# Local attention in blocks of 64 queries by 96 keys, with a step of 32 slots

## The reference

```python
qkv = x @ Wqkv                                   # 128 -> 3 * 1024, 16 heads of 64; x is token-shifted
q = l2norm(q) * qs;  k = l2norm(k) * ksc         # then rotary tables with a scale per token
# local attention, window 32: query i sees keys i-32 .. i
mask = (it < jb) | (it > jb + w) | (jb == -1)
sim = einsum('bhwie,bhwje->bhwij', bq, bk2) * QK_SCALE
attn = softmax(where(mask, -big, sim), -1)
out = einsum('bhwij,bhwje->bhwie', attn, bv2)
x = x + out @ Wo
# feed-forward: layernorm, W1 (128 -> 2 * 341), a * gelu(gate), W2, residual
```

## Time and profile before

| | |
|---|---|
| median of three runs | 5323.7 us |
| profiled execution, span | 5323.2 us |
| PE, DVE busy | 4734.5 us (89%), 4646.5 us (87%) |
| ACT, POOL busy | 3909.8 us (73%), 3520.9 us (66%) |
| phase A, B, C (about) | 0 to 508, 508 to 4600, 4600 to 5323 us |

### The profile page before, as it was taken

The page is one execution under the profiler, slowest core; times in us unless marked ns, Lnnn a source line. Parts: engine busy times, 40 slices in busy tenths (PEclk is TensorE's granted clock), DMA queues, the critical chain, the costliest instruction groups (busy, mean ns, idle before and its releaser), DMA issues. The chain is left out here.

```text
span 5323.2 us, 107258 instructions
## 1 busy us (share of the span) xinstructions
PE 4734.5 (89%) x32878; PEld 3336.2 (63%) x32878; DVE 4646.5 (87%) x8811; ACT 3909.8 (73%) x11543; POOL 3520.9 (66%) x2504
## 2 busy tenths in 40 slices
PE   6996899989999899999999999999989999688887
PEld 4554666666666666666666666666667666445553
DVE  4776999989999999999999999999989999388887
ACT  2554787878778787787778877787878878577774
POOL 0111777778778777777777777787878788145454
PEclk9998999999999999999999999999999999888888
DMA  1000000000000000000000000000000000000000
GB/s 23 6 5 27 1 1 1 0 7 8 9 1 0 6 8 9 1 0 6 8 9 0 1 4 10 9 0 1 0 14 3 0 0 0 5 3 3 3 3 5
DMA packets 35433, 26.55 MB, mean 5 GB/s; under 512 B 11203, under 2 KB 29190, under 8 KB 35078
## 3 DMA queue, kind: packets, MB, share of 16 engines
q1 hardware_dynamic: 26302, 22.22, 1.4%
q10 hardware_dynamic: 8776, 0.45, 0.1%
HBM read 20.56 MB, written 2.10 MB: 4 GB/s over the span
## 5 line engine op out<-in xcount | busy, mean ns | idle before, releaser
L1286 POOL TENSOR_TENSOR b_w<-b_w,b_vt 128x512 f32<-128x512 f32 x768 | 1176.2, 1536 | 850.8 <-DVE b_ss L1196 542.7
L1290 POOL TENSOR_TENSOR b_rn<-b_ssm,all_neg_half 128x16 f32<-128x16 f32 x384 | 1128.1, 2938 | 32.0
L1085 ACT ACTIVATE b_Pr<-ps,b_nm 128x128 f32<-128x128 f32 x1536 | 570.3, 371 | 523.9 <-DVE b_nm L1250 522.9
L1244 DVE TENSOR_TENSOR b_Pr<-b_Pr,b_rinv 128x640 f32<-128x640 f32 x768 | 738.0, 961 | 26.4
L965 PE MATMUL ps<-b_Whi,b_xlo 128*128 128x512 f32 x1152 | 578.3, 502 | 202.3 <-DVE b_vt L1194 166.1
L1250 DVE TENSOR_REDUCE b_nm<-ps 128x4 f32<-128x640 f32 x768 | 628.9, 819 | 58.4 <-PE ps L946 50.8
L1106 ACT ACTIVATE b_sq<-ps 128x512 f32<-128x512 f32 x768 | 471.4, 614 | 259.6 <-PE ps L967 210.4
L1087 ACT ACTIVATE b_Pr<-ps,b_nm 128x160 f32<-128x160 f32 x1536 | 610.3, 397 | 0.0
L1192 DVE TENSOR_TENSOR b_w<-ps,until_b_rotab 128x512 f32<-128x512 f32 x768 | 523.9, 682 | 20.4 <-ACT b_sq L1106 17.5
L1194 DVE TENSOR_TENSOR b_vt<-ps,until_b_rotab 128x512 f32<-128x512 f32 x768 | 522.5, 680 | 0.0
L1196 DVE TENSOR_REDUCE b_ss<-b_sq 128x8 f32<-128x512 f32 x768 | 519.2, 676 | 0.0
(11 more groups left out here) (269 smaller groups left out, 11969.3 us busy)
## 6 DMA issues: line engine op xcount, KB each, us to landing
b_Wraw<-in_L_ffn_Wqkv SPq DMA_DIRECT2D x36, 256.0 KB, 2.8
b_Wo<-in_L_ffn_Wo SPq DMA_DIRECT2D x6, 512.0 KB, 4.2
a_xtok<-in_L_attn_hidden_states SPq DMA_DIRECT2D x16, 128.0 KB, 2.1
out<-c_xout SPq DMA_DIRECT2D x16, 128.0 KB, 1.8
b_W<-in_L_ffn_W SPq DMA_DIRECT2D x6, 341.0 KB, 2.9
setup_wmod<-in_L_wmod SPq DMA_DIRECT2D x2, 384.0 KB
b_W<-in_L_ffn_W SPq DMA_DIRECT2D x6, 128.0 KB
setup_rot<-in_rot SPq DMA_DIRECT2D x1, 256.0 KB
```

What stands on the lines that cost most here:

```text
L1085: nc.scalar.activation(s.Pr[:, p % 4, j, 0, WIN:], ps[:, S_BANK[j], WIN:KEYS], ACT.Exp, bias=s.nm[:, h, 0:1], accum_out=s.ssum[:, h, 0:1])
L1244: nc.vector.tensor_tensor(rows, rows, inverse, ALU.mult).then_inc(s.scaled, 1)
L1286: nc.gpsimd.tensor_tensor(rows, rows, s.vt[:, i % 4], ALU.add).then_inc(s.pool_add, 1)
L1290: nc.gpsimd.tensor_tensor(s.rn[:, j], s.ssm[:, j], g.neg_half[:, 0:HB], ALU.pow).then_inc(s.pool_r, 1)
```

## The change

The attention is tiled as four blocks of 64 queries by 96 keys (BLK = 64, KEYS = 96) instead of two of 128 by 160. Two pairs of heads make a round; an item has 4 rounds. Masks and scores go to 64x64 corners of the PE array: head j picks the row half and the S bank, block b the column half and the partitions of PSUM. Maximum, reciprocal and multiplication are one instruction a round, over 768 columns. The DVE transpose is gone; each block's 96 keys are transposed whole by PE. As a block's keys now need their values on partitions 0 to 95, V is held by block: ACT copies a piece into Vraw and SP spreads it by transfers, 10 an item. V has one buffer instead of two. SP's program becomes part of the stepped loop, with its weight loads in it. A step has SLOTS = 32 slots, and all slot tables of phase B are new. Phase C's source is the same.

```diff
+BLK = 64
+KEYS = BLK + WIN
+NBLK = NT // BLK
+MASK_COLS = 2 * TT * KEYS
...
+ROUNDS = HPAIRS // 2
+HALF = INNER // 2
+SLOTS = 32
+ROUND = SLOTS // ROUNDS
+QK_SLOT = {0: (0, 0), 3: (0, 2), 6: (1, 0), 8: (1, 2), 15: (0, 1), 17: (0, 3), 22: (1, 1), 24: (1, 3)}
+V_SLOT = {14: (0, 4), 20: (1, 4), 29: (0, 5), 31: (1, 5)}
...
+SCORE_LAG, EXP_LAG, SCALE_LAG, TURN_LAG, VALUE_LAG, COPY_LAG = 0, (2, 5), 8, (9, 11), 15, 14
...
+            def spread_values(item, half, tt):
+                cols = slice(half * HALF, (half + 1) * HALF)
+                sp.wait_ge(s.act_front, N_PIECES * item + PIECE.index(VALUE[2 * half + tt]) + 1)
+                if tt == 0 and not (isinstance(item, int) and item == 0):
+                    sp.sem_inc(s.spent, 1)
+                    sp.wait_ge(s.pv_done, ROUNDS * (item - 1) + 2 * (half + 1))
+                if tt == 0:
+                    sp.dma_start(s.V[WIN:KEYS, 0, cols], s.Vraw[0:BLK, tt]).then_inc(s.v_in[tt], 16)
+                    sp.dma_start(s.V[0:KEYS, 1, cols], s.Vraw[BLK - WIN:P, tt]).then_inc(s.v_in[tt], 16)
+                    sp.dma_start(s.V[0:WIN, 2, cols], s.Vraw[P - WIN:P, tt]).then_inc(s.v_in[tt], 16)
+                else:
+                    sp.dma_start(s.V[WIN:KEYS, 2, cols], s.Vraw[0:BLK, tt]).then_inc(s.v_in[tt], 16)
+                    sp.dma_start(s.V[0:KEYS, 3, cols], s.Vraw[BLK - WIN:P, tt]).then_inc(s.v_in[tt], 16)
...
+                def scores(r):
...
+                    for b in range(2):
+                        for j in range(2):
+                            side, block = slice(j * DB, (j + 1) * DB), slice(b * BLK, (b + 1) * BLK)
+                            nc.tensor.matmul(ps[block, S_BANK[j], 0:MASK_COLS], g.ident_bf[side, side], g.mask_bf[side, b], start=True, stop=False,
+                                             skip_group_check=True)
+                    for a in range(2):
+                        q, k = s.qkT[:, pa, 2 * r + a], s.qkT[:, pa, INNER // P + 2 * r + a]
+                        for tt in range(TT):
+                            for b in range(2):
+                                start = tt * P + b * BLK
+                                hidden = WIN if start == 0 else 0
+                                at = (a * TT + tt) * KEYS + hidden
+                                for j in range(2):
+                                    side = slice(j * DB, (j + 1) * DB)
+                                    last = nc.tensor.matmul(ps[b * BLK:(b + 1) * BLK, S_BANK[j], at:at + KEYS - hidden], q[side, start:start + BLK],
+                                                            k[side, start - WIN + hidden:start + BLK], start=False, stop=True, skip_group_check=True)
...
+                def values(item, r):
...
+                    for a in range(2):
+                        for blk in range(NBLK):
+                            for j in range(2):
+                                head = slice((4 * r + 2 * a + j) * DB, (4 * r + 2 * a + j + 1) * DB)
+                                at = j * TT * P + blk * BLK
+                                last = nc.tensor.matmul(ps[j * DB:(j + 1) * DB, O_BANK, a * NT + blk * BLK:a * NT + (blk + 1) * BLK],
+                                                        s.V[KEY_ROWS, blk, head], s.PT[KEY_ROWS, a, at:at + BLK], start=True, stop=True, skip_group_check=True)
...
-                        nc.vector.transpose(s.PT[P - WIN:P, p % 2, :, P:KEYS], s.Pr[0:WIN, p % 4, :, 1, 0:WIN]).then_inc(s.before_ready, 1)
```

More of the change, by code:

```diff
@@ L781, in spare_of_before, with latest, phase_b_steps @@
         return i % 2, self.halves + i // 2
-def phase_b_steps(engine, body):
+    def latest(self, uses, before):
+        found = {}
+        for use in uses:
+            bank, count = self.spare_of_before(use) if before else self.spare(use)
+            i = (self.uses_before if before else self.uses).index(use)
+            if bank not in found or i > found[bank][0]:
+                found[bank] = (i, count)
+        return [(bank, count) for bank, (_, count) in sorted(found.items())]
+def phase_b_steps(engine, body, between=None):
     def whole(n):
@@ L867, in load_chunks @@
                 for k in pieces:
-                    wait(sp, s.w_ready, WCHUNKS * l + k + 1 - RAW)
                     c = CHUNKS[k]
[L870 to L885, removed]
+                    converted = WCHUNKS * l + k + 1 - RAW
@@ L890, in _ @@
             sp.wait_ge(s.w2_in, 32 * DEPTH)
+            for loaded, times in zip(s.v_in, SPREAD):
+                sp.wait_ge(loaded, 16 * times * 2 * ITEMS)
         @block.tensor
@@ L967, in body @@
                         nc.tensor.matmul(ps[:, F_BANK[k % 2]], s.xhi[:, pf, rows], s.Whi[:, cols], start=False, stop=True).then_inc(s.proj_done, 1)
[L968 to L977 removed]
+                    item, r = round_at(step, slot, SCORE_LAG)
+                    if r is not None:
+                        scores(r)
+                    item, r = round_at(step, slot, VALUE_LAG)
+                    if r is not None:
+                        values(item, r)
                     if step.tail is not None:
@@ L1107, in body @@
                         else:
[L1108 to L1113 removed]
+                            i = VALUE.index(slot)
@@ L1114, in body @@
+                            wait(act, s.v_in[i % 2], 16 * SPREAD[i % 2] * (2 * f + i // 2))
+                            nc.scalar.activation(s.Vraw[:, i % 2], ps[:, F_BANK[k % 2]], ACT.Copy).then_inc(s.act_front, 1)
+                    item, r = round_at(step, slot, COPY_LAG)
+                    if r is not None:
+                        act.wait_ge(s.pv_done, ROUNDS * item + r + 1)
+                        if r == 0 and step.tail is not None:
                             b, uses = step.spare(("wo", 0))
@@ new lines, in body @@
+                    read_spare(slot - READ_LAG)
+                    for a in range(2):
+                        item, r = round_at(step, slot, EXP_LAG[a])
+                        if r is not None:
+                            exps(item, r, a)
+                    for a in range(2):
+                        item, r = round_at(step, slot, TURN_LAG[a])
+                        if r is not None:
+                            p = 2 * r + a
+                            act.wait_ge(s.t_done, HPAIRS * item + p + 1)
+                            wait(act, s.pv_done, ROUNDS * item + r)
+                            nc.scalar.activation(s.PT[KEY_ROWS, p % 2], ps[KEY_ROWS, T_BANK], ACT.Copy).then_inc(s.pt_ready, 1)
```

305 lines of the change are left out of this document (155 added, 150 removed).

## The result

The changed kernel takes 5203.77 us (median of 4 runs, 5194.01 to 5206.96), against 5323.84 us for the kernel before in the same session: a ratio of 0.9772 [0.9758, 0.9786], 120 us faster where 349 were forecast. It lies in the range of 4850 to 5250, near its upper end. Its profiled execution spans 5205.1 us.

The account below looks back on a forecast made before the run. PE and DVE, 93% busy each, set phase B's step together. 5323.2 - 442 (steps) - 20 (layer changes) + 5 (start) + 108 (phase C) = 4974, stated as 4975 us; forecast 4880 to 5090, wider range 4850 to 5250.

Parts of the forecast that it names:

- The attention on PE: Phase B, PE: four corners at once, a round of 2.3 us, 5.2 us less an item, PE 33.0 a step.
- Rival A: Phase B, PE: small matmuls don't keep the pace of their columns; 5240, 5345 or some 5920 us; chance 0.16.
- DVE, ACT, POOL: Phase B, busy time a step: DVE falls to 30.4 us and leaves the bound, ACT 31.9, POOL 32.0.
- The step: Phase B: PE's 33.0 us at 90% gives a step of 36.7 us, 4.6 x 96 = 442 us saved.
- Rival B: Phase B: four engines wait for each other in a fixed slot order, 38.9 us a step, 5195 us; chance 0.20.
- Transfers and the change of layer: Phase B: V's transfers on SP priced at 0; five layer changes cost about 10 us instead of 14, 20 saved.
- Rival D: Phase B: V's transfers land in 8 us, not 3, +3 us a step, 5260 us; chance 0.05.
- The start: Start of the kernel: SP waits for the zeroing and the mask table grows, +5 us once.
- Phase C: Phase C: SLOTS = 32 moves sums ahead of the next step's spreads, 15 seams x 7.0 = +105 us, up to +140.
- rival C: Phase C absorbs the moved sums, so the kernel takes 4865 us; chance 0.07.

Follow-up runs that it names:

- both repairs: The changed kernel with PE's inner loop of phase B written out and phase C's loops at 16 slots: 4945.65 us (0.9295).

## Why the prediction was right or wrong

**The attention on PE: right, in the overlap and in the price.** Timeline of PE in the kernel after:

```profile
1003.29 0.36 PE L1004 MATMUL ps<-until_b_mask_bf,until_b_ident_bf 64*64 64x384 bf16 x4
1003.48 0.83 PE L1015 MATMUL ps<-b_qkT 64*64 64x64 f32 x32
1004.24 0.66 PE L989 MATMUL ps<-all_ident,b_w 128*128 128x128 f32 x4
```

Masks and scores take 0.95 us (0.97 forecast), values 1.08 (1.03; 1036.22 to 1037.30 above). Rival A falls: 32 value matmuls in 1.08 us are 34 ns each, quicker than the 46 ns of the earlier trace rows. The 62 ns that the Trainium skill ("TensorE: Matmul & The Clock Gate", section "Wait — 56ns, not 53.3ns?") gives with hardware decode off would have made it 1.98 us; the trace doesn't agree with that case.

**DVE, ACT, POOL: right in the main.** With both repairs, two steps of 75 us hold PE 68.83, DVE 63.51, ACT 62.82 and POOL 61.02: 34.4, 31.8, 31.4 and 30.5 a step, where 33.0, 30.4, 31.9 and 32.0 were forecast. The stretch is 1.1 us longer than two steps; over exactly two (73.9 us) PE has 33.9 and DVE 31.2. Most of PE's excess is the clock: that stretch has 0.98 granted, and without the Gelu, at 1.00, PE has 66.49 in two steps, 33.2 each, nearly the 33.0 of the forecast.

On DVE a product of 768 columns takes 961 ns (1.1 forecast) and a maximum 956 (0.87). The base of 961 for 640 columns was a mean over products of 824 to 1746 ns, whose median is 826; and 0.87 isn't 0.819 with the 0.13 that I priced for 128 columns. The two errors nearly cancel. The excess lies in lines that the change doesn't touch: the scaling of 1024 columns (L1203 before) goes from 1345 to 1816 ns on average, twice a step, and the second copy to b_xhi (L1149 before) from 291 to 1308 ns, once a step. What stretches them was not tried.

**The step: right for what it covered.** Ordinary steps without a jump take 38.1 and 35.8, 36.96 on average; 36.7 was forecast. Two errors meet in this: PE is busier, and 92% of the step rather than 90%. Rival B (lock-step at 38.9) is out, though 5195 is nearest to the result: it is near for another reason.

**The failed step: a term that the sum lacked.** I counted the instructions (281 matmuls to 409 a step) only as a pace, and not as the length of a loop's body. I had the outer loop's branch in the trace of before too, with the body of a whole layer behind it:

```profile
L798 PEldq COMPARE_BRANCH  x5: 79/3590/3727, 1328.5 to 4035.2; - x5
```

3.6 us beside the inner one's 0.21 says that a long body pays. 30 jumps, each with 3.3 us of idle and a stretch at 1.2 GHz behind it, make the 150.7 us that the written-out loop gives back, two thirds of the 229 us between 4975 and 5203.8.

**Transfers and the change of layer: right in the mechanism named, wrong in the order of a queue.** The transfers of V land in time: ACT's copy into Vraw waits 61.6 us in all for PE, and never for a transfer. Rival D is out (count, KB, median us to landing):

```profile
b_V<-b_Vraw SPq DMA_DIRECT2D x384, 192.0 KB, 2.6
b_V<-b_Vraw SPq DMA_DIRECT2D x384, 128.0 KB, 2.3
b_V<-b_Vraw SPq DMA_DIRECT2D x192, 64.0 KB, 2.2
```

But "behind SP's new waits stand only the weight loads, and each is awaited 6 slots or more later" is false where it counts. The wait of the transfers of the step before ends at slot 7 of the step that needs the chunks from slot 8 on. A change of layer was to cost 10 us more than ordinary steps. The four steps 53.0, 36.6, 38.4, 38.2 and the first of the loop, 42.5, make 208.7, 24 more than five ordinary ones; the next three make 22.5 to 23 more, the last, which has no outer jump behind it, 18. That is 110 us over five changes where 50 were forecast: 60 lost. With the chunks from ACT's queue and the outer jump gone, the five steps make 46.6 + 36.2 + 38.4 + 37.2 + 37.8 = 196.2, 11 more; over all five changes it is 54, and the forecast's 50 is nearly met.

**The account of phase B.** 237.5 us are missing (462 less 224.5). The inner jumps are 150.7 (155.5 in phase B between the two profiled executions), the layers' changes 60, and 0.26 us in each of 94 steps is 24; a last step of only 30.3 us gives 7 back. That makes 228 to 233. The rest is rounding in the forecast: 95 steps of 36.7 and five changes of 10 are 3536.5 us, where 3992.8 - 462 is 3530.8. The start, priced at +5, went the other way (the first step begins 2.6 us earlier), which brings the whole miss to some 230.

**Slips in the sums.** By its own terms rival B's step of 38.9 us gives 5186, not 5195, and rival A's round of 3.4 us a PE of 37.4, not 37.6. The sum uses 108 us for phase C where its working has 105. None of them moves the forecast by more than 3 us.

**Phase C: right in mechanism and size.** The sums now stand in a row at the end of a step, ahead of the next step's spreads, and POOL's first product waits for ACT's copy, as forecast; PE and POOL in phase C of the kernel after:

```profile
4941.81 8.85 PE L1742 MATMUL ps<-c_bu,all_ident 128*128 128x512 f32 x20
4950.59 0.73 PE L1701 MATMUL ps<-c_xbc,c_sel 64*128 64x256 f32 x4
```
```profile
4904.03 5.12 POOL L1596 TENSOR_TENSOR c_bu<-c_du,c_rows 128x512 f32<-128x512 f32 x4 [9.78 <-ACT c_rows L1629]
...
4951.80 5.13 POOL L1596 TENSOR_TENSOR c_bu<-c_du,c_rows 128x512 f32<-128x512 f32 x4 [9.78 <-ACT c_rows L1629]
```

The period is 47.8 us (48 forecast) where it was 41.0, which over 16 items is 109 us, and the wait of the earlier trace rows, 2.97 us, is now 9.78. Undone it gives 109.0, done to the kernel before it takes 110: rival C is out.

## What to carry to other kernels

When a change splits instructions into smaller ones, count the instructions of the longest loop body on that engine: a branch that cost 0.2 us can come to cost 3.5 us and a slow clock behind it, and writing the loop out for that one engine takes it back. When transfers are added to a queue, ask of everything behind them on that queue, across the step's edge, when the last wait ahead of it ends. Where TensorE stands idle, read the granted clock of the stretch behind the idle too: in the changed kernel a jump cost 3.3 us of idle, and PE's work 2.5 us more behind it. And a constant that two stages share changes both.

The best kernel of these runs (loops written out for TensorE, 16 slots in phase C, chunks from ACT's queue) takes 4889.76 us, 8.1% under the kernel before, where the change alone gives 2.3%.

## What the runs showed that I had not expected

PE's jump is cheap at 1522 instructions in the body (0.21 us) and dear at 1778 (3.49) and 2512 (3.65). Instructions in a straight line cost nothing visible at nearly as many packets fetched (344 for 425). And leaving out the two table loads of 1.28 us around each Gelu, with a copy of the Gelu's length in its place, gives back 132 us over 48 calls, 2.7 us each: half of it is PE's wait for the copies behind, a third PE's slower clock behind that wait.
